# A four-row ring of inputs for TensorE, filled by a GpSimd copy in place of a DMA inside SBUF

## What is computed

```python
x = x + _L0_conv_ref(_gn(x), W_qkv, b_qkv)
# inside _L0_conv_ref, for every image b and row g:
qkv = einsum('bglc,dc->bgld', x, W_qkv) + b_qkv      # 384 = q, k, v of two heads
score = einsum('bghlc,bghmc->bghlm', q, k) / sqrt(C)
out = einsum('bghlm,bghmc->bghlc', softmax(score), v)
```

## Time and profile before

| | |
|---|---|
| Median of 3 runs | 4365.6 us (4364.17 to 4367.62) |
| Profiled execution, its own time | 4368.04 us |
| Its span in the profile | 4365.9 us |
| Mean granted TensorE clock | 0.963 |
| Busy: TensorE, VectorE, ScalarE, POOL | 91%, 84%, 70%, 41% |
| HBM read and written | 134.42 MB, 134.22 MB |
| Moved by all DMAs | 944.11 MB |

### The profile page before, as it was taken

One profiled execution on the slowest core, in us unless ns is written; L12 is line 12 of the kernel. 1 busy time (PEld: TensorE's weight loads), 2 busy tenths in 40 slices (PEclk: granted clock), 3 DMA queues, 4 the chain that ended last, 5 costly groups with the idle time before them and its releaser, 6 DMA issues.

```text
span 4365.9 us, 144522 instructions
## 1 busy us (share of the span) xinstructions
PE 3961.3 (91%) x44133; PEld 3009.3 (69%) x44133; DVE 3673.0 (84%) x7138; ACT 3037.9 (70%) x8193; POOL 1781.8 (41%) x2065
## 2 busy tenths in 40 slices
PE   4898989989899898998989989899898988989998
PEld 3676767667676676766767667676676766767776
DVE  6896978879788797987979879798797987979987
ACT  3676767667676676766767667677676766767776
POOL 1443434434344343443434434344343433434444
PEclk9999999999999999999999999999999999999999
DMA  7999999999999999999999999999999999999999
GB/s 190 221 206 241 210 227 220 187 241 210 227 219 189 241 210 231 216 189 240 209 234 216 185 243 210 229 216 190 245 210 231 220 194 235 209 242 210 202 209 196
DMA packets 2508947, 944.11 MB, mean 216 GB/s; under 512 B 2180544, under 2 KB 2443072, under 8 KB 2508608
## 3 DMA queue, kind: packets, MB, share of 16 engines
q1 hardware_dynamic: 2384768, 814.22, 90.3%
q10 hardware_dynamic: 123840, 125.83, 9.1%
HBM read 134.42 MB, written 134.22 MB: 62 GB/s over the span
## 4 chain that ended last, share of the span: by engine, by line
PE 55%; DMA 13%; issue 12%; DVE 9%; SPq 7%; POOL 1%; ACT 1%; DVEq 1%; POOLq 0%; ACTq 0%
PE s_bank L297 15%; PE qk_bank L275 15%; PE o_bank L313 12%; DMA pt_hi<-p_hi 12%; PE v_bank L285 7%; PE xt_bank L267 4%; DVE neg_max L427 3%; SPq L227 3%; SPq L231 3%; PE v_bank L282 2%; DVE v_lo L440 1%; POOL p_hi L598 1%; DVE o_norm L453 1%; DVE bn L458 1%; DMA pt_lo<-p_lo 1%
## 5 line engine op out<-in xcount | busy, mean ns | idle before, releaser
L607 POOL TENSOR_TENSOR y_ring<-image,o_norm 128x256 f32<-128x256 f32 x1024 | 742.6, 725 | 2268.0 <-DVE o_norm L453 2268.0
L392 ACT ACTIVATE prob<-s_bank,neg_max 128x256 f32<-128x256 f32 x4096 | 1612.7, 492 | 69.8 <-issue 60.8
L373 ACT ACTIVATE qk<-qk_bank,b_in 128x256 f32<-128x256 f32 x2048 | 859.1, 471 | 950.8 <-PE qk_bank L275 949.5
L427 DVE TENSOR_REDUCE neg_max<-s_bank 128x2 f32<-128x512 f32 x2048 | 1313.2, 684 | 63.8 <-PE s_bank L297 62.8
L297 PE MATMUL s_bank<-qk 64*128 64x256 f32 x8192 | 1221.2, 418 | 45.5 <-issue 44.7
L434 DVE SCALAR_TENSOR_TENSOR p_lo<-prob,p_hi 128x1024 f16<-128x1024 f32 x1024 | 1239.5, 1210 | 4.9 <-POOL p_hi L598 1.4
L598 POOL TENSOR_SCALAR p_hi<-prob 128x1024 f16<-128x1024 f32 x1024 | 1068.6, 1044 | 312.4 <-DMA pt_hi<-p_hi 238.7
L275 PE MATMUL qk_bank<-xc,w_norm 128*128 128x256 f32 x4096 | 1190.1, 414 | 0.0
L313 PE MATMUL o_bank<-v_hi,pt_lo 128*128 128x65 f16 x8192 | 868.2, 195 | 282.0 <-DMA pt_hi<-p_hi 226.3
L275 PEld LDWEIGHTS qk_bank<-xc,w_norm 128*128 128x128 f32 x4096 | 714.1, 194 | 413.6 <-issue 342.9
L313 PEld LDWEIGHTS o_bank<-v_hi,pt_lo 128*128 128x128 f16 x8192 | 767.3, 99 | 304.1 <-DMA pt_hi<-p_hi 235.4
(11 more groups left out here) (71 smaller groups left out, 1922.8 us busy)
## 6 DMA issues: line engine op xcount, KB each, us to landing
x_ring<-image SPq DMA_DIRECT2D x512, 256.0 KB, 2.6
out_dram<-y_ring SPq DMA_DIRECT2D x512, 256.0 KB, 2.4
image<-in_x_dram ACTq DMA_DIRECT2D x60, 2048.0 KB, 9.6
pt_hi<-p_hi SPq DMA_TRANSPOSE x1024, 3.3
pt_lo<-p_lo SPq DMA_TRANSPOSE x1024, 3.2
image<-in_x_dram SPq DMA_DIRECT2D x4, 2048.0 KB, 16.5
w_in<-in_L_conv_W_qkv_dram SPq DMA_DIRECT2D x1, 192.0 KB, 2.4
b_in<-in_L_conv_b_qkv_dram SPq DMA_DIRECT2D x3, 0.5 KB, 2.1
```

What stands on the lines that cost most here:

```text
L373: ins = act.activation(qk[:, v % 2, t, :], qk_bank[:, t * TOK:(t + 1) * TOK], ACT.Identity, bias=b_in[:, t:t + 1])
L392: ins = act.activation(prob[:, m, c:c + TOK], s_bank[m][h][:, a * TOK:(a + 1) * TOK], ACT.Exp, bias=neg_max[:, m, h, a:a + 1])
L427: dve.tensor_reduce(neg_max[:, m, h, :], s_bank[m][h][:, :].rearrange("p (a k) -> p a k", a=J), AX.X, ALU.max, negate=True).then_inc(max_d ...
L607: pool.tensor_tensor(y_ring[:, m, :], image[:, par, bass.ds(row, 1), :].rearrange("p a c -> p (a c)"), o_norm[:, v % 2, :, :].rearrange("p ...
```

## The change

The ring's refill moves from SyncE's queue to POOL. It becomes one POOL `tensor_copy` per row (128 partitions by 256 float32) in place of one DMA per two rows, and stands between `finish` and `p_high` in POOL's order. The semaphore becomes one that counts rows.

```diff
-        ring_in = [sem(f"ring_in{i}") for i in range(2)]
+        ring_in = sem("ring_in")
...
         @block.sync
-            def refill(base, v, at):
-                par, row = at
-                if v % 2:
-                    return
-                k = v % 4 // 2
-                if known_below(base, 2 - v):
-                    sp.wait_ge(first_in[0], 16)
-                if not known_below(base, 4 - v):
-                    sp.wait_ge(xt_done, base + (v - 2))
-                sp.dma_start(x_ring[:, 2 * k:2 * k + 2, :], image[:, par, bass.ds(row, 2), :]).then_inc(ring_in[k], 16)
...
             def order(run, next_image):
                 run(-2, transpose_low)
-                run(+5, refill)
                 run(-6, store)
                 run(-1, transpose_high)
...
             def x_transpose(base, v, at):
                 m = v % 4
-                pe.wait_ge(ring_in[m // 2], base * 4 + 16 * (v // 4 + 1))
+                pe.wait_ge(ring_in, base + (v + 1))
...
         @block.gpsimd
+            def refill(base, v, at):
+                par, row = at
+                if not known_below(base, 4 - v):
+                    wait_apart(pool, xt_done, base + (v - 3))
+                pool.tensor_copy(x_ring[:, v % 4, :],
+                                 image[:, par, bass.ds(row, 1), :].rearrange("p a c -> p (a c)")).then_inc(ring_in, 1)
...
+            pool.wait_ge(first_in[0], 16)
+
             def order(run, next_image):
                 run(-4, finish)
+                run(+5, refill)
                 run(-1, p_high)
```

## The result

The change makes the kernel slower: 4481.6 us (median of 4 runs, 4474.49 to 4486.27) against 4364.9 us before, a ratio of 1.027 (95% interval 1.025 to 1.029). The forecast was 4411 us, slower with a chance of 0.74. The direction is right and the measured time lies in the range, but the loss is 117 us where 45 were forecast.

The account below looks back on a forecast made before the run. Several limits near 3.7 us a row were seen, with the POOL-VectorE loop becoming the binding one. 4365.9 + 79 (measuring rows) + 20 (statistics rows) - 54 (loads) = 4411 us; 8 in 10 range 4330 to 4530.

Parts of the forecast that it names:

- closed loop: POOL and VectorE wait on each other once per row: 3.57 us, growing to 3.88 with the copy and binding.
- handover at 0.04: Sign: from the end of `p_hi` to the start of `p_lo`, 0.04 us instead of 0.19 in nearly all rows.
- 0.31 - 0.15 = 0.16 us more a row: Measuring rows: loop growth less its slack; over 31 rows of 16 images, +79 us.
- R: Growth of the loop by the copy between `y_ring` and `p_hi` on POOL: 0.31 us, bounds 0.23 to 0.69.
- The slack: Spare time of the loop per row before the change: 3.57 us needed against 3.72 between `p_lo` starts, so 0.15 us.
- The statistics rows: Rows 47 to 59 of 15 images, six with small VectorE instructions inside the loop: +1.35 us an image, +20 us.
- The loads: Load stretch, 60 image loads: removing refill DMAs saves half their time, 0.9 us a load, -54 us (-114 to +18).
- The rule of turns per packet: DMA engines alternate between queues packet by packet, so removing refills could save 3.3 us a load; sum 4267 us.
- The other rows: Some 92 rows outside the loads, at the image's edges, already longer than 3.74 us: nothing, at most +15 us.
- The dear copy: Rival: POOL's copy costs what `y_ring` costs, 0.69 us, 0.54 more a row; 4719 us, chance 0.08.
- nothing to be measured: Rival: the loop's slack swallows a copy under 0.18 us and the loads gain nothing; 4366 us, chance 0.06.
- The rival on the other side: Load stretch gives back more than the loop takes, from 1.65 us a load; 4315 us at 2.5, chance 0.18.

Follow-up runs that it names:

- the copy alone: Kernel before with its DMA refill kept, plus the POOL copy in the change's place into a spare ring nobody reads: 4508.5 us, ratio 1.033.
- two copies: The change with a second POOL copy of the same row into a spare ring right ahead of the real one: 4767.9 us, ratio 1.092.
- the half copy: The change with only 128 of each row's 256 elements copied after the first four rows: 4403.6 us, ratio 1.008.
- the removal alone: Kernel before with the DMA refill left out after the first four rows and no copy in its place: 4314.4 us, ratio 0.989.

## Why the prediction was right or wrong

**The mechanism was right, and the size of the loss was not.** The closed loop through `p_lo`, `o_norm`, `y_ring` and `p_hi` was nearly the bound already and became it. The handover at 0.04, `p_lo` waiting, the copy 0.67 after `y_ring`, idle time on TensorE and VectorE and a lower DMA share (0.82, towards 0.75 foretold) are all there, and the copy alone gives the loss while a place outside the loop takes it away.

**The step that failed in size is "0.31 - 0.15 = 0.16 us more a row".** It is a small difference of two numbers that I read each from too little. Measured it is 0.24.
- R was 0.31 by a line through a memset of 4 elements; it is 0.34. Over rows 20 to 45 of all images the mean time from `y_ring` to `p_hi` is 0.695 before, 1.034 after, and 1.377 with two copies. The copy takes 397 ns, not 344: a copy has a longer foot than a memset. 496 rows x 0.03 = 15 us.
- The slack was 0.15, taken from one row; it is 0.10 on the mean. Over the same rows the handover falls from 0.187 to 0.062 and not to 0.04, since one row in four, at the edge of the hardware loop, keeps 0.15. And `o_norm` starts 1.143 after `p_lo` instead of 1.117. That makes 0.125 - 0.026 = 0.10. The row that I picked is none of those at the edge. 496 x 0.05 = 25 us.

Together these are 40 of the 41 us between 79 and 120. Each error was a few hundredths of a microsecond, and together they made the difference half as large again. The other figure for the copy that the prediction names, 0.38 us, came nearer to 0.397 by luck: spread over 256 elements it is 1.5 ns each with no foot, where the half copy shows 0.84 ns each on a foot of 182 ns.

**The statistics rows**: +30 against +20. With the measured 3.98 us in place of 3.90 the prediction's own sum gives 12 x 3.98 + 2.0 - 47.45 = 2.3 an image, +35. So the same two causes more than explain it, and the estimate of 2.0 for the small instructions was somewhat high.

**The loads**: -34 against -54. Half of the refills' time was a guess between bounds, and 20 us of the error come from it. With whole loads the refill is worth 0.45 us each by itself and 0.56 in the change, inside my bounds of -0.3 to 1.9. The rule of turns per packet in the Trainium skill (DMA: Bandwidth & Descriptors, section "Queues, rings and completion order") gave an estimate of 3.3 us a load in the prediction; no run here comes near it.

**The other rows**: -6 against nothing. That costing hid 28 us which the removal alone gives in these rows; the copy alone changed them by 2.

**The rivals.** The dear copy (4719 us) is out at 397 ns; nothing to be measured is out. The rival on the other side, that the loads pay for the loop, needed 1.65 us a load and had 0.56. With halved loads the refill is worth nearly that much (1.4), which I didn't foresee.

**The copy's own waits** cost nothing in the loop, as predicted: the profile puts 37.9 us on its wait for the transposition, three times in all, nearly all of it at the start of the program.

## What to carry to other kernels

An engine's idle time is room only if it isn't waiting for the result of its own earlier work: follow the wait back, and if it comes round to the same engine, everything put on that engine between the links is paid in each round once the loop's slack (0.10 us here) is used up, however low its share. Put the work where the engine waits instead, beside an instruction that it doesn't lengthen; the same copy cost 120 us of measuring rows in one place and nothing in the other. And when a forecast is a difference of two near numbers, take both from means over many rows: a slack read from one row was 0.15 us where the mean was 0.10.

## What the runs showed of the hardware

- POOL's copy of 256 float32 per partition takes 397 ns, of 128 it takes 290; start to start the copy and the next instruction are 0.36 us apart.
- When POOL's copy and VectorE's `p_lo` overlap by 0.15 us or less, nothing is lost; an overlap of 0.26 us lengthened `p_lo` by 0.10. Beside `o_norm`, which reads its large input from PSUM, an overlap left both times as they were (480 and 397 ns on the mean).
- Cutting a 2 MB load in two changed nothing (ratio 1.0008) while the DMA engines also copied inside SBUF, and won about 50 us without that (ratio 0.978 against 0.9885).
